# Rotary attention: the two value products of a key tile issued in one beat of every two instead of one in each

## The chip, the cores and the metric
The kernel runs on one core of a Trainium2 chip. The metric is the device time of one execution in microseconds (us); lower is better. Before the change three runs gave 2062.24, 2063.32 and 2064.73 us, median 2063.32 us.

## What is computed
The input x has 16 batches of 512 tokens with 128 features. Four blocks follow one another, each added to x: a causal attention, a feed-forward block, an attention with rotary positions ("rotary attention", the one that changes), and the same feed-forward block again. Each starts from a layer norm. The rotary attention is, cut to what matters:

```
q, k, v = (x @ Wq.T + bq), (x @ Wk.T + bk), (x @ Wv.T + bv)   # 16 heads of 8
q, k = rope(q, k)
scores = einsum('bhnd,bhmd->bhnm', q, k) / sqrt(8)
attn = softmax(scores)                        # no mask: all 512 x 512 of a head
out = einsum('bhnm,bhmd->bhnd', attn, v) @ Wo.T + bo
```

## The kernel before, in words
The whole of x stays on the chip. Each attention is a software pipeline over the batches: step n works on several batches at once, each in another stage. A step has 32 **beats** (`BEATS`, 4 groups of 4 heads times 8 beats). In every beat TensorE (PE) executes in the order given by `"order": "SMWX"`:

- S, `scores` (line 1007): the scores of batch n-2 for one pair of heads and one tile of 128 keys, two matmuls of 50 rows by 512 queries, side by side in the upper and the lower half of the array. Here they are called S(i,0) and S(i,1) for beat i. Each writes a PSUM bank of its own.
- M, `maxes` (line 1025): the same products the other way round for batch n-1, two matmuls, from which VectorE (DVE) takes the maxima over the keys (`max_of`, line 882).
- W, `weigh` (line 1065): a **value block**. Four matmuls, one for each head of the group, in four column strips of 32; each multiplies 128 keys of the probabilities (256 of the 512 queries) with the values and a column of ones (9 columns, float32), and adds to `ps_out`. Float32 matmuls stand as two records each in the trace, so a block is "x8".
- X, `misc_work`: at a few beats of a step, projections of q, k, v (lines 1106, 1109), the output product (line 1135), transposes of the normed x (line 1092) and of the maxima (line 1076).

ScalarE (ACT) takes the exponential of each score bank in order (line 993: two per beat, `prob`), and copies `ps_out` to SBUF once a group of heads is complete (`group_out`, line 956, `o_raw`).

The banks set the waits. The scores have `SCORE_BANKS = 3` banks, taken in turn by S(i,0), S(i,1), S(i+1,0), S(i+1,1) and so on (`act_bank_free`): so S(i+1,1) takes the bank of S(i,0) and waits for its exponential. Transposes at beats 3, 19 and 23 take turns too. The maxima have two pairs of banks: M of beat i waits for DVE's reduction of beat i-2. `ps_out` is one bank: the first value block of a group waits for the copy of the group before (`s["o_raw"]` in `weigh`). PE, ACT and DVE each execute their instructions in program order.

`ROTARY_AT` is the table that puts the parts at their beats. `"weigh"` gives, for the eight value blocks of a group G, the beat counted from 8G. Block 2j and block 2j+1 are the two halves of the queries (0 to 255, 256 to 511) of key tile j, and both read the probabilities of beats 2j and 2j+1; beats past 31 fall in the next step. There are 8 probability buffers (`PROBS`): the exponential of beat i waits for the last block that reads beat i-8.

Of the kernel before, what the change touches and what calls it, by code (L numbers as in the profile page):

```python
# [328 lines left out]
def norm_apply(dve, m, s, b):  # L329
# [3 lines left out]
    for t in range(T):  # L333
# [7 lines left out]
             "P_nm0": 10, "P_o": 1, "D_stats": 6, "D_clear": 9, "D_q": 14, "D_k": 4, "A_v": 6, "D_bias": 6, "D_inv": 12,  # L341
             "D_proj": 9, "A_nm1": 2, "A_nm0": 14, "A_xT": 10, "order": "MSWX"}
ROTARY_AT = {"k": 3, "nm1": 3, "v": 15, "proj": 14, "xT": 19, "nm0": 23, "q": 23,
             "weigh": (4, 5, 6, 7, 8, 9, 10, 11), "out": 12, "P_nm1": 8, "P_norm": 15, "P_v": 13, "P_bias": 15,
             "P_q1": 27, "P_q2": 31, "P_k1": 9, "P_k2": 13, "P_nm0": 19, "P_o": 0, "D_stats": 16, "D_clear": 18,
             "D_q": 24, "D_k": 4, "A_v": 16, "D_bias": 2, "D_inv": 15, "D_proj": 15, "A_nm1": 4,
             "A_nm0": 24, "A_xT": 20, "order": "SMWX"}
# [1291 lines left out]
```

## Time and profile before
| | |
|---|---|
| median of three runs | 2063.32 us |
| the profiled execution, its time | 2065.22 us |
| its span on the chip | 2063.5 us |
| granted TensorE clock, mean over the span | 0.962 |
| rotary attention in the main loop | about 995 to 1697 us |
| one step of it (one batch) | 43.4 us |
| busy over the span | PE 92%, DVE 83%, ACT 72%, POOL (GpSimd) 57% |

An engine's busy time is the union of its instructions. Matmuls are pipelined, and the end of each is modelled, so the distance between the starts of two instructions says more than the length of one. Idle time in brackets stands before an instruction, with what released it. Step n of the rotary loop does the scores for batch n-2: steps 2 to 16 have S, M and W, step 17 has S and W alone, and the next feed-forward block begins beside it.

### The profile page before, as it was taken

The page shows a single profiled execution, that of the slowest core. Times are in us where ns is not written, and L with a number is a line of the kernel's source. Part 1 is how long each engine was busy: PE and PEld are TensorE (multiplying, and loading weights), DVE is VectorE, ACT ScalarE, POOL GpSimd, SP SyncE. Part 2 cuts the span into 40 slices and gives each one's busy share as a digit, 9 for nine tenths or more (in the row PEclk, how much of TensorE's full clock was granted, in tenths as well). Part 3 has the DMA queues.
Part 4 walks back from the last instruction along what each step waited for, and adds up shares of the span by engine and source line. Part 5 has one row for each costly group of instructions (what it writes and reads, how often), then busy time and mean ns, then how long its engine had stood idle before and what let it go on. Part 6 is the DMA issues. An engine that isn't in the chain of part 4 may idle for free.

```text
span 2063.5 us, 42740 instructions
## 1 busy us (share of the span) xinstructions
PE 1888.6 (92%) x16132; PEld 966.2 (47%) x16132; DVE 1702.8 (83%) x2312; ACT 1478.0 (72%) x2641; POOL 1175.8 (57%) x1615
## 2 busy tenths in 40 slices
PE   3899999999889999986899999999999989999998
PEld 1333444444357777764222222222222227777776
DVE  4889898898658888876899999999999918888883
ACT  1478788788756666652698888888888876666665
POOL 6777788877446555677444454454553015555654
PEclk6799999999989999998799999999999989999999
DMA  7455656655110000014334444444444010000000
GB/s 180 99 120 134 131 125 140 126 121 119 25 40 1 0 1 1 1 27 101 88 90 101 99 105 107 95 100 95 101 111 95 14 19 12 11 16 11 11 16 16
DMA packets 107892, 144.81 MB, mean 70 GB/s; under 512 B 19105, under 2 KB 87458, under 8 KB 101538
## 3 DMA queue, kind: packets, MB, share of 16 engines
q1 hardware_dynamic: 107682, 142.01, 30.3%
q8 instruction: 132, 2.16, 0.5%
q14 instruction: 78, 0.64, 0.1%
HBM read 67.52 MB, written 55.58 MB: 60 GB/s over the span
## 4 chain that ended last, share of the span: by engine, by line
PE 59%; POOL 15%; issue 8%; ACT 8%; DVE 6%; DMA 2%; SPq 1%; POOLq 0%; another core or an unknown queue 0%; ACTq 0%; DVEq 0%
PE ps_score L1446 21%; PE ps_out L1065 12%; PE ps_score L1007 7%; ACT prob L993 6%; PE ps_max L1446 5%; PE ps_max L1025 5%; DVE negmax L882 3%; POOL xhat L324 3%; POOL prob L728 3%; PE ps_out L1446 3%; PE ps_max L1106 2%; POOL rstd L318 2%; POOL rest L693 1%; ACT o_raw L956 1%; POOL parts L700 1%
## 5 line engine op out<-in xcount | busy, mean ns | idle before, releaser
L993 ACT ACTIVATE prob<-ps_score 128x512 f32<-128x512 f32 x1664 | 900.4, 598 | 171.8 <-PE ps_score L1007 151.4
L882 DVE TENSOR_REDUCE negmax<-ps_max 128x2 f32<-128x1024 f32 (+1 forms) x896 | 905.6, 1066 | 90.7 <-PE ps_max L1042 47.9
L1065 PE MATMUL ps_out<-prob,v_aug 128*9 128x256 f32 (+2 forms) x6656 | 508.9, 386 | 30.9 <-ACT o_raw L956 20.4
L1446 PE MATMUL ps_score<-h,w_hi 128*128 128x512 f32 x2048 | 502.8, 399 | 9.4 <-POOL h L1224 8.2
L1446 PEld LDWEIGHTS ps_score<-h,w_hi 128*128 128x128 f32 x2048 | 383.3, 189 | 104.3 <-POOL h L1224 10.8
L1025 PE MATMUL ps_max<-stack_k,stack_q 48*128 48x512 bf16 (+3 forms) x2048 | 342.6, 353 | 46.6 <-DVE negmax L882 29.3
L1007 PE MATMUL ps_score<-stack_q,stack_k 50*128 50x512 bf16 (+3 forms) x2048 | 351.6, 347 | 31.0 <-ACT prob L993 23.1
L1212 POOL TENSOR_TENSOR h<-h3f,h 128x512 fp32r<-128x512 f32 x128 | 192.5, 1514 | 127.9 <-ACT h L1358 127.8
L728 POOL TENSOR_SCALAR_AFFINE_SELECT prob<-prob 128x256 f32<-128x256 f32 (+1 forms) x448 | 187.8, 440 | 117.7 <-ACT prob L993 117.3
L1065 PEld LDWEIGHTS ps_out<-prob,v_aug 128*9 128x9 f32 x6656 | 105.8, 89 | 306.0 <-ACT prob L993 153.9
L1007 PEld LDWEIGHTS ps_score<-stack_q,stack_k 50*128 50x128 bf16 x2048 | 103.7, 93 | 273.1 <-ACT prob L993 201.6
L1212 POOL TENSOR_TENSOR h<-h2f,h 128x512 fp32r<-128x512 f32 x128 | 172.7, 1351 | 68.3 <-ACT h L1358 68.3
L680 POOL TENSOR_TENSOR turned<-turned,rope 128x512 f32<-128x512 f32 x31 | 39.5, 1275 | 283.2 <-DMA turned<-qf 283.2
L1025 PEld LDWEIGHTS ps_max<-stack_k,stack_q 48*128 48x128 bf16 x2048 | 87.7, 95 | 200.8 <-DVE negmax L882 97.3
L1352 ACT ACTIVATE h3f<-ps_score,s_col 128x512 f32<-128x512 f32 x128 | 87.7, 685 | 110.8 <-PE ps_score L1446 104.2
L1352 ACT ACTIVATE h2f<-ps_score,s_col 128x512 f32<-128x512 f32 x128 | 88.2, 689 | 96.2 <-PE ps_score L1446 89.6
L1266 DVE CAST h<-h1f 128x512 fp32r<-128x512 f32 x120 | 124.9, 1041 | 37.5 <-PE ps_score L1446 36.4
L1446 PE MATMUL ps_max<-ffn_xT,w_hi 128*128 128x512 f32 x512 | 144.9, 415 | 3.4 <-DVE ffn_xT L1273 2.5
L334 DVE TENSOR_SCALAR xhat<-x,mv,rstd 128x128 f32<-128x128 f32 x128 | 95.5, 806 | 44.1 <-POOL rstd L306 44.1
L1253 DVE SCALAR_TENSOR_TENSOR ut<-tanh,ps_max 128x512 f32<-128x512 f32 x128 | 87.0, 680 | 53.1 <-ACT tanh L1369 50.6
L1268 DVE TENSOR_TENSOR h<-h1f,h 128x512 fp32r<-128x512 f32 x120 | 114.8, 957 | 4.1
L1446 PEld LDWEIGHTS ps_max<-ffn_xT,w_hi 128*128 128x128 f32 x512 | 93.4, 193 | 36.4 <-DVE ffn_xT L1273 15.5
(116 smaller groups left out, 2129.5 us busy)
## 6 DMA issues: line engine op xcount, KB each, us to landing
d_stack<-parts SPq DMA_DIRECT2D x64, 384.0 KB, 2.6
stack_q<-d_stack SPq DMA_DIRECT2D x64, 384.0 KB, 5.7
stack_k<-d_stack SPq DMA_DIRECT2D x64, 384.0 KB, 6.0
d_stack<-parts SPq DMA_DIRECT2D x64, 256.0 KB, 2.9
d_stack<-parts SPq DMA_DIRECT2D x64, 128.0 KB, 2.7
o_num<-o_raw SPq DMA_DIRECT2D x128, 64.0 KB
o_rden<-d_rden SPq DMA_DIRECT2D x128, 64.0 KB
turned<-qf SPq DMA_DIRECT2D x64, 128.0 KB, 2.4
```

The source lines that it names most:

```text
L334: last = dve.tensor_scalar(m["xhat"][:, t, :], m["x"][:, b % B, t, :], m["mv"][:, t, 0:1], m["rstd"][:, t:t + 1], ALU.subtract, ALU.mult)
L728: last = pool.affine_select(out=tri, in_=tri, compare_op=ALU.is_ge, fill=0.0, base=0, pattern=[[0, tri.shape[1]], [1, P]], channel_multipl ...
L882: last = dve.tensor_reduce(m["negmax"][:, t, :, p], banks[:, :, at:at + w], AX.X, ALU.max, negate=True)
L993: act.activation(prob(b, i)[:, o], act_bank("score", 2 * i + o), ACT.Exp).then_inc(s["prob"], 1)
L1007: mm = pe.matmul(act_bank("score", 2 * i + o)[:, at:at + w], m["stack_k"][c][rows, p, P * j:P * (j + 1)], m["stack_q"][c][rows, p, S - w:S ...
L1025: last = pe.matmul(to[:, o, at:at + w], m["stack_q"][c][rows, p, P * t:P * (t + 1)], m["stack_k"][c][rows, p, 0:w], start=(piece == 0), st ...
L1065: last = pe.matmul(m["ps_out"][32 * g:32 * g + HD + 1, out:out + w], m["v_aug"][b % VALUES][:, j, 4 * G + g, :], prob(b, beat)[:, g % 2, l ...
L1212: pool.tensor_tensor(h[k][:, 1, f], hf[k][:, f % 2], h[k][:, 0, f], ALU.subtract).then_inc(s[f"h{k}"], 1)
L1266: dve.tensor_copy(h[1][:, 0, f], h1f[:, f % 2]).then_inc(s["h1_hi"], 1)
L1268: dve.tensor_tensor(h[1][:, 1, f], h1f[:, f % 2], h[1][:, 0, f], ALU.subtract).then_inc(s["h1"], 1)
L1352: act.activation(hf[k][:, f % 2], m["ps_hid"][:, f % 2], ACT.Gelu, scale=m["s_col"][:, k, f:f + 1]).then_inc(s[f"h{k}f"], 1)
L1446: mm = pe.matmul(to, w[:, cols], moving(part), start=begin and i == 0, stop=last and i == len(pairs) - 1)
```

## The change
One row of the table:

```diff
 ROTARY_AT = {"k": 3, "nm1": 3, "v": 15, "proj": 14, "xT": 19, "nm0": 23, "q": 23,
-             "weigh": (4, 5, 6, 7, 8, 9, 10, 11), "out": 12, "P_nm1": 8, "P_norm": 15, "P_v": 13, "P_bias": 15,
+             "weigh": (5, 5, 7, 7, 9, 9, 11, 11), "out": 12, "P_nm1": 8, "P_norm": 15, "P_v": 13, "P_bias": 15,
              "P_q1": 27, "P_q2": 31, "P_k1": 9, "P_k2": 13, "P_nm0": 19, "P_o": 0, "D_stats": 16, "D_clear": 18,
```

The even blocks (0, 2, 4, 6) of each group go one beat later, behind S and M of the odd beat, directly in front of the odd block, which stays. Even beats have S and M (and X) alone; odd beats have S, M and two value blocks. The number of instructions of each kind stays. A group's first block goes from beat 8G+4 to beat 8G+5; the last one stays at 8G+11, and the copy of a group's output stays at ACT's beat 8G+12.

## Rows read from the trace of the kernel before
**Rows 1.** The page's first part: busy us (share of the span) xinstructions.
```profile
PE 1888.6 (92%) x16132; PEld 966.2 (47%) x16132; DVE 1702.8 (83%) x2312; ACT 1478.0 (72%) x2641; POOL 1175.8 (57%) x1615
```
**Rows 2.** Busy time by stretch, one step: PE, PEld, DVE, ACT, POOL, clock, DMA share, GB/s.
```profile
1306.82:1350.27 43.45, 41.14 (x418) 11.71 (x416) 40.41 (x45) 38.25 (x73) 21.34 (x28) 1.00 0.46 101
```
**Rows 3.** Who waited for whom, 1306.33 to 1349.79: us in total, times, longest.
```profile
ACT prob L993 <- PE ps_score L1007: 3.1, 5, 1.1
...
PE ps_out L1065 <- ACT o_raw L956: 1.4, 3, 0.6
...
PE ps_score L1007 <- ACT prob L993: 0.6, 1, 0.6
...
PE ps_score L1092 <- POOL xhat L324: 0.4, 1, 0.4
```
**Rows 4.** Order of time, PE, beats 4 and 5: start, length, instruction.
```profile
1306.33 0.39 PE L1007 MATMUL ps_score<-stack_q,stack_k 50*128 50x512 bf16 x2
1306.56 0.38 PE L1025 MATMUL ps_max<-stack_k,stack_q 48*128 48x512 bf16 x2
1306.87 0.62 PE L1065 MATMUL ps_out<-prob,v_aug 128*9 128x256 f32 x8
1307.42 0.43 PE L1007 MATMUL ps_score<-stack_q,stack_k 50*128 50x512 bf16 x2
...
1308.00 0.62 PE L1065 MATMUL ps_out<-prob,v_aug 128*9 128x256 f32 x8
1308.55 0.39 PE L1007 MATMUL ps_score<-stack_q,stack_k 50*128 50x512 bf16 x2
```
**Rows 5.** Order of time, ACT, beats 4 to 11.
```profile
1306.82 8.84 ACT L993 ACTIVATE prob<-ps_score 128x512 f32<-128x512 f32 x16 [0.36 <-PE ps_score L1007]
```
**Rows 6.** Order of time, beats 16 and 17, after the v projection.
```profile
1322.23 0.39 PE L1007 MATMUL ps_score<-stack_q,stack_k 50*128 50x512 bf16 x2
...
1322.83 2.06 ACT L993 ACTIVATE prob<-ps_score 128x512 f32<-128x512 f32 x4
...
1323.32 0.54 PE L1007 MATMUL ps_score<-stack_q,stack_k 50*128 50x512 bf16 x2
...
1324.01 0.62 PE L1065 MATMUL ps_out<-prob,v_aug 128*9 128x256 f32 x8
```
**Rows 7.** Order of time, PE after the loop: four value blocks with nothing between.
```profile
1693.73 1.91 PE L1065 MATMUL ps_out<-prob,v_aug 128*9 128x256 f32 x32
...
1695.57 1.20 PE L1446 MATMUL ps_max<-ffn_xT,w_hi 128*128 128x512 f32 x4
```
**Rows 8.** Order of time, beats 11 to 14, around a group's copy.
```profile
1314.67 0.62 PE L1065 MATMUL ps_out<-prob,v_aug 128*9 128x256 f32 x8
...
1315.54 0.60 ACT L956 ACTIVATE o_raw<-ps_out 128x512 f32<-128x512 f32 x1
...
1316.20 0.62 PE L1065 MATMUL ps_out<-prob,v_aug 128*9 128x256 f32 x8 [0.37 <-ACT o_raw L956]
...
1317.84 0.43 PE L1007 MATMUL ps_score<-stack_q,stack_k 50*128 50x512 bf16 x2
```
**Rows 9.** Order of time, PE, output product of beat 14, scores of 15.
```profile
1318.97 1.16 PE L1135 MATMUL ps_max<-weights,oT 128*128 128x128 f32 x8
...
1320.06 0.39 PE L1007 MATMUL ps_score<-stack_q,stack_k 50*128 50x512 bf16 x2
```
**Rows 10.** Order of time, PE, the first scores of the next step.
```profile
1344.10 0.39 PE L1007 MATMUL ps_score<-stack_q,stack_k 50*128 50x512 bf16 x2 [0.56 <-ACT prob L993]
```
**Rows 11.** Order of time, DVE, ten reductions on end.
```profile
1350.56 11.52 DVE L882 TENSOR_REDUCE negmax<-ps_max 128x2 f32<-128x1024 f32 x10
```
**Rows 12.** Order of time, PE, a beat of step 17 (no M).
```profile
1645.44 0.63 PE L1007 MATMUL ps_score<-stack_q,stack_k 50*128 50x512 bf16 x2
```
**Rows 13.** Order of time, PE at the lower clock, S of two successive beats.
```profile
1001.76 0.61 PE L1007 MATMUL ps_score<-stack_q,stack_k 50*128 50x512 bf16 x2
...
1003.70 0.61 PE L1007 MATMUL ps_score<-stack_q,stack_k 50*128 50x512 bf16 x2
```

## The prediction
> **What bounds the kernel now.** I read the page's busy shares first: PE leads with 92% of the span [rows 1]. The diff touches only the rotary attention, so next I read one step of it in the view by stretches: of 43.45 us PE is busy 41.14, DVE 40.41, ACT 38.25, at a granted clock of 1.00, the level of 2.4 GHz [rows 2]. Three engines are within 3 us of each other, so a share says little about which sets the pace; the order of time has to. The waits of one step are small: ACT waits 3.1 us for scores, PE 1.4 us for group copies, 0.6 us for an exponential at the step's start, 0.4 us for the normed x [rows 3].
>
> In the order of time a plain beat on PE is S to M 0.23, M to W 0.31, W to the next S 0.55; two beats take 1308.55 - 1306.33 = 2.22 us [rows 4]. A second loop is as long, and the view of waits hardly shows it. S(4,0) starts at 1306.33, its exponential at 1306.82, 0.49 later [rows 4, 5]. An exponential lasts 0.60. S(5,1) takes the bank of S(4,0): its exponential ends at 1306.82 + 0.60 = 1307.42, and S of beat 5, started at 1307.42, is 0.43 long where its neighbours are 0.39: its second matmul came 0.04 later [rows 4]. So the loop "S(i,0), its exponential, S(i+1,1)" takes 0.49 + 0.60 + 0.04, about 1.12 us, whatever PE does in between. Beats 16 and 17 prove it: the exponential of S(16,0) is held back by the v copy to 1322.83 and ends at 1323.43; S(17,0) starts at 1323.32, S ends 0.15 later than usual (0.54 against 0.39), so S(17,1) started about 1323.47, 0.04 after that end, and W of the beat went with it, to 1324.01, 0.54 after S(17,1) [rows 6]. A beat that lacks M shows the same: S is 0.63 long, 0.24 of it waiting [rows 12].
>
> **The change part by part.** No instruction is added or removed.
>
> *The even beat loses its value block (0.55 us).* S(e,0) at 0, M at 0.23, S(o,0) at about 0.45. S(o,1) then waits for the exponential of S(e,0): it cannot start before 1.12. M of the odd beat and both value blocks stand behind it on PE. So of the 0.55 us taken out here nothing is gained; the even beat's distance to S(o,1) stays 1.12 to 1.13 (today 1307.46 - 1306.33).
>
> *The odd beat has two value blocks.* From S(o,1) to the first W 0.54 [rows 4, 6]. Two blocks on end are not in a rotary beat of the trace. The nearest row: four on end take 1695.57 - 1693.73 = 1.84, that is 0.43 each and 0.12 once for the way out of them [rows 7]; two are 0.98. From below I take 0.86 (the way out hidden), from above two single ones, 2 x 0.55 = 1.10. I take 0.98, the same operation in the same shapes.
>
> *A plain pair of beats* is then 1.12 + 0.54 + 0.98 = 2.64 us (2.52 to 2.76) against 2.22: **+0.41**. The 0.12 that adjacency saves goes under the wait. At the pair's end: the four exponentials follow one another 0.49 apart (four in 2.06, [rows 6]) from 0.48, and end at 2.55, before the next S at 2.64, whose first exponential starts at 3.12. DVE needs 1.15 a beat (ten in 11.52, [rows 11]), 2.30 a pair, and is not late. 16 pairs a step: +6.6 us.
>
> *What goes back.* (a) The group copies. The first block of a group now comes a beat after the copy's place, so PE's wait at it goes: 1.4 us in three, at beats 12, 20 and 28 [rows 3]. But the copy sits in front of the exponential of the even beat, and begins 0.25 us after W has ended (1314.67 + 0.62 to 1315.54, [rows 8]): from the next S that is 0.32, plus 0.48 for the copy, so the exponential starts at 0.80 and not 0.48, and the loop carries these 0.32. Today the pair of beats 12 and 13 is 1317.84 - 1315.22 = 2.62 (1315.22 is W at 1314.67 and 0.55); it becomes 2.96. That is +0.34 and not +0.41, for three pairs -0.2. (b) The output product in beat 14, 1.09 us from 1318.97 to 1320.06 [rows 9], falls in an even beat, where PE is waiting: S(15,0) at 0.23 + 0.31 + 1.09 = 1.63 instead of 1.12, so it costs 0.51 of its 1.09: -0.58. (c) At the step's start S(0,0) waits for the last exponential of beat 31, 0.56 on PE [rows 10]. The pair of beats 30 and 31 is now longer than its exponentials (2.55, and 0.15 from the end to S), so 0.5 of that wait is swallowed: -0.5. (d) The wait for the normed x, 0.4 [rows 3], ends by POOL's own work, which the change does not lengthen; PE arrives later: -0.4. All other X work stands behind odd beats and is added to a pair as before. What is late next after (a) and (c) is the same exponential of the even beat. SP, the DMAs and POOL keep their order; no instruction passes another there, and with POOL at 21.34 of 43.45 [rows 2] a longer step gives them room.
>
> A step: 6.6 - 0.2 - 0.6 - 0.5 - 0.4 = **+4.9**, nearer to +4.8 with unrounded terms; 43.4 becomes 48.2.
>
> *All steps.* Steps 3 to 14: 12 x 4.8 = 57.6. Step 2 has 14 such pairs: +4.0. Steps 15 and 16 have no transpose of x, so (d) is missing: 2 x 5.2. Step 17 has no M: a pair becomes 2.64 - 0.22 = 2.42 against at most 2.24 (two turns of the loop) and about 2.0 where the beats run by PE; over 14 pairs +2.5 to +5.9, part of it under waits there: I take +4. The sum is +76 us. The profiled execution took 2065.22 us (span 2063.5); it becomes 2141. Against the median of 2063.32 that is 2139 us.
>
> *The clock.* Today PE has 2.3 us idle in a step at a granted 1.00 [rows 2]; it will have some 0.3 us idle in each pair, 4 to 5 us more in a step. At the lower level a rotary beat takes 1003.70 - 1001.76 = 1.94 us [rows 13], so a pair would be about 4.0 against 2.64. No stretch of the rotary loop shows the clock falling at such gaps, and gaps below 1 us stand in it at 1.00; I cost it at nothing in the forecast and keep it as a rival.
>
> **The rivals.**
>
> *The clock falls (slower still).* If PE, with a gap in each pair, spends a tenth to a quarter of the loop at 1.2 GHz, then each low pair costs 1.36 us more: 250 pairs x 1.36 x 0.1 to 0.25 = +34 to +85, so 2173 to 2224 us. For it: the gaps come regularly. Against: each is short, and PE is still busy about 89%. The Trainium skill, page "TensorE: Matmul & The Clock Gate", section "A second HAM failure mode: psum-queue depth-cycling", describes just this pattern, 512-column bf16 matmuls that cycle through PSUM banks with small idle times between groups, and says that the clock then swings between its two levels. The present loop cycles three banks at 1.00 [rows 2], so the trace does not bear the rule out at today's gaps; at the new ones no row shows it.
>
> *Adjacency saves nothing:* two blocks take 1.10, a pair 2.76, and +0.12 x 250 = +30: 2169 us. Against it stand rows 7.
>
> *PE alone sets the pace (faster).* If S(o,1) did not have to wait, a pair on PE would be 0.22 + 0.22 + 0.22 + 0.31 + 0.98 = 1.95, and DVE would bound it with 2.30. The waits for group copies and the step's start go too; a step is then DVE's 40.41 busy and about 1 us that it still waits for q, 41.4 instead of 43.4: -2.0 in 15.5 steps, -31 us, 2032 us. It decides from the point where the exponential of S(e,0) is over when S(o,0) is issued, at 0.45. For it: PE leads the busy shares, and 0.12 us goes at each way out of the value blocks. Against: that exponential ends at 1.08, by rows 4 to 6.
>
> *The value blocks' place does not matter* (the wait for the bank is in fact shorter, and a pair stays about 2.22 to 2.30): -0.1 to +0.5% of the time, near 2063. Against it the same rows.
>
> **How the numbers follow.** Forecast 0.78; clock 0.08; no saving 0.05; PE sets the pace 0.06; no matter 0.03. The forecast's own range: the value blocks 0.86 to 1.10, so ±0.12 x 250 = ±30, and step 17 ±2; the upper side meets the rival with 1.10. I take 2112 to 2170, which leaves out the faster cases and the worse half of the clock's. A change of 0.2% (4 us) is about what can be told from none. Faster by more 0.07, within 0.02, slower 0.91.
>
> **What would show it.** Right: rotary steps of 48.2 us (47 to 50); on ACT, groups of four exponentials, 2.07 long, with about 0.57 idle before each for scores; on PE, S of odd beats held by ACT's exponential for some 0.3 us, fifteen times a step, and x16 value groups 0.98 from start to next S; no wait of a value block for the group copy; DVE idle about 7 us in a step; clock 1.00. Wrong: exponentials without a gap, or a step under 43.4 (the bank wait does not bind), a granted clock under 0.98 in the loop (the clock rival), x16 groups of 1.10.

## The result and the profile after
The changed kernel takes 2144.61 us (median of four runs, 2144.46 to 2144.65) against 2064.03 us for the kernel before beside it: the ratio is 1.0391, 95% interval 1.0377 to 1.0405. It is 80.6 us slower; 2139 us were forecast, in a range of 2112 to 2170. The span of the profiled execution went from 2063.5 to 2142.7 us.

First the page's busy shares, which answer to [rows 1], and the view by stretches for one step, from one v copy to the next, which answers to [rows 2].

```profile
PE 1914.8 (89%) x16132; PEld 1004.8 (47%) x16132; DVE 1716.2 (80%) x2312; ACT 1462.5 (68%) x2641; POOL 1178.0 (55%) x1615
...
1067.77:1116.01 48.24, 42.73 (x418) 14.20 (x417) 41.12 (x43) 37.24 (x73) 21.37 (x28) 1.00 0.39 89
```

A step has the same 418 matmul records and takes 48.24 us instead of 43.45. The busy times move by 1.6 us at most; what grew is the idle time of each engine: PE from 2.3 to 5.5 us, DVE from 3.0 to 7.1, ACT from 5.2 to 11.0. They do not stand together: PE is busy while ACT waits for it, and ACT while PE waits. The waits of the same step, to be read beside [rows 3]:

```profile
ACT prob L993 <- PE ps_score L1007: 7.7, 13, 0.8
PE ps_score L1007 <- ACT prob L993: 5.4, 15, 0.6
DVE negmax L882 <- PE ps_max L1025: 5.0, 15, 0.9
```

PE and ACT wait for each other: PE 15 times a step for an exponential (5.4 us; it was 0.6), ACT 7.7 us for scores (it was 3.1). DVE waits 5.0 us for the products M. The wait of a value block for a group copy, 1.4 us in [rows 3], is gone. The order of time shows one pair of beats; it answers to [rows 4].

```profile
1392.95 0.39 PE L1007 MATMUL ps_score<-stack_q,stack_k 50*128 50x512 bf16 x2
1393.17 0.38 PE L1025 MATMUL ps_max<-stack_k,stack_q 48*128 48x512 bf16 x2
1393.39 0.38 PE L1007 MATMUL ps_score<-stack_q,stack_k 50*128 50x512 bf16 x1
1393.43 2.06 ACT L993 ACTIVATE prob<-ps_score 128x512 f32<-128x512 f32 x4 [0.59 <-PE ps_score L1007]
1393.60 2.36 DVE L882 TENSOR_REDUCE negmax<-ps_max 128x2 f32<-128x1024 f32 x2 [0.30 <-PE ps_max L1025]
1394.08 0.39 PE L1007 MATMUL ps_score<-stack_q,stack_k 50*128 50x512 bf16 x1 [0.31 <-ACT prob L993]
1394.09 0.60 PE L1025 MATMUL ps_max<-stack_k,stack_q 48*128 48x512 bf16 x2
1394.62 1.05 PE L1065 MATMUL ps_out<-prob,v_aug 128*9 128x256 f32 x16
1395.60 0.39 PE L1007 MATMUL ps_score<-stack_q,stack_k 50*128 50x512 bf16 x2
```

Read it down. S of the even beat at 1392.95, S(o,0) at 1393.39, and S(o,1), a group of its own now, at 1394.08: the view puts 0.31 idle before it and names the exponential. The first exponential began at 1393.43 and ended 0.60 later, at 1394.03. From S(e,0) to S(o,1) it is 1.13. Two value blocks follow at +0.54, and the next S 0.98 after them, so adjacency does save its 0.12. The pair is 1395.60 - 1392.95 = 2.65. ACT has groups of four exponentials with 0.59 idle before each, where [rows 5] has sixteen on end.

### The profile page after: what moved, and what is told of

Its sections match the earlier page's. It is cut to its first block, busy times and chain, and to the rows that moved or that the text cites. A ratio compares the mean times of both kernels' runs of the same rounds, so it can differ in the third digit from the quotient of the medians.

```text
span 2142.7 us, 42740 instructions
## 1 busy us (share of the span) xinstructions
PE 1914.8 (89%) x16132; PEld 1004.8 (47%) x16132; DVE 1716.2 (80%) x2312; ACT 1462.5 (68%) x2641; POOL 1178.0 (55%) x1615
## 4 chain that ended last, share of the span: by engine, by line
PE 66%; POOL 11%; ACT 10%; issue 7%; DVE 4%; DMA 1%; SPq 0%; POOLq 0%; ACTq 0%; DVEq 0%
PE ps_score L1446 20%; PE ps_out L1065 16%; PE ps_score L1007 10%; ACT prob L993 8%; PE ps_max L1446 5%; PE ps_max L1025 5%; POOL prob L728 3%; PE ps_max L1106 2%; PE ps_out L1446 2%; DVE negmax L882 2%; POOL xhat L324 1%; ACT o_raw L956 1%; POOL rest L693 1%; POOL parts L700 1%; POOL rstd L318 1%
## 5 line engine op out<-in xcount | busy, mean ns | idle before, releaser
L993 ACT ACTIVATE prob<-ps_score 128x512 f32<-128x512 f32 x1664 | 877.2, 603 | 234.3 <-PE ps_score L1007 224.2
L882 DVE TENSOR_REDUCE negmax<-ps_max 128x2 f32<-128x1024 f32 (+1 forms) x896 | 921.0, 1067 | 133.1 <-PE ps_max L1025 83.1
L1007 PE MATMUL ps_score<-stack_q,stack_k 50*128 50x512 bf16 (+3 forms) x2048 | 426.0, 347 | 109.4 <-ACT prob L993 100.2
L1065 PE MATMUL ps_out<-prob,v_aug 128*9 128x256 f32 (+2 forms) x6656 | 465.0, 387 | 9.6 <-POOL prob L728 9.6
L1025 PE MATMUL ps_max<-stack_k,stack_q 48*128 48x512 bf16 (+3 forms) x2048 | 379.8, 352 | 46.8 <-DVE negmax L882 30.2
L1007 PEld LDWEIGHTS ps_score<-stack_q,stack_k 50*128 50x128 bf16 x2048 | 114.5, 94 | 391.0 <-ACT prob L993 302.0
L1065 PEld LDWEIGHTS ps_out<-prob,v_aug 128*9 128x9 f32 x6656 | 132.3, 90 | 232.2 <-issue 81.3
```

The source lines that it names most:

```text
L882: last = dve.tensor_reduce(m["negmax"][:, t, :, p], banks[:, :, at:at + w], AX.X, ALU.max, negate=True)
L993: act.activation(prob(b, i)[:, o], act_bank("score", 2 * i + o), ACT.Exp).then_inc(s["prob"], 1)
L1007: mm = pe.matmul(act_bank("score", 2 * i + o)[:, at:at + w], m["stack_k"][c][rows, p, P * j:P * (j + 1)], m["stack_q"][c][rows, p, S - w:S ...
L1025: last = pe.matmul(to[:, o, at:at + w], m["stack_q"][c][rows, p, P * t:P * (t + 1)], m["stack_k"][c][rows, p, 0:w], start=(piece == 0), st ...
L1065: last = pe.matmul(m["ps_out"][32 * g:32 * g + HD + 1, out:out + w], m["v_aug"][b % VALUES][:, j, 4 * G + g, :], prob(b, beat)[:, g % 2, l ...
```

## The experiments
Each was timed beside the kernel before on its own chip; the medians of before were 2061.3 and 2061.4 us there. Ratios are to these. "Step" is the mean of 13 steps, from one v copy to the next.

| kernel | us | ratio, 95% interval | step, us |
|---|---|---|---|
| before | 2064.03 | | 43.46 |
| changed | 2144.61 | 1.0391 (1.0377 to 1.0405) | 48.24 |
| e1, changed, S(o,1) behind M | 2100.02 | 1.0193 (1.0176 to 1.0210) | 45.42 |
| e2, before, S(i,1) behind M | 2060.30 | 0.9992 (0.9982 to 1.0001) | 43.25 |
| e3, pairs in the even beat | 2154.31 | 1.0454 (1.0433 to 1.0476) | 48.66 |
| e4, one pair in four | 2086.30 | 1.0122 (1.0105 to 1.0139) | 45.16 |
| e5, before, short exponentials | 2043.63 | 0.9914 (0.9898 to 0.9931) | 42.54 |
| e6, changed, short exponentials | 2071.81 | 1.0049 (1.0032 to 1.0065) | 43.62 |
| e7, changed, last batch as before | 2132.30 | 1.0352 (1.0335 to 1.0369) | |
| e8, before, last batch in pairs | 2071.81 | 1.0050 (1.0033 to 1.0066) | |

**e1: what stands behind the wait.** The theory: the loop from S(e,0) over its exponential to S(o,1) holds its length, and everything PE has behind S(o,1) is added. The rival: two value blocks on end are the cost. The order in which the four matmuls of S and M are issued tells them apart. The edit in words:

```diff
-    S(i,0), S(i,1), M(upper half), M(lower half)      # scores(), then maxes()
+    S(i,0), M(lower half), M(upper half), S(i,1)      # one function, steps 2 to 16
```

> The changed kernel, with the four matmuls of S and M of a beat in another order: S(i,0), M for the lower half, M for the upper half, S(i,1). Same work, same banks. Theory (the loop S(e,0), its exponential, S(o,1) holds 1.12 us of the pair, and what stands behind S(o,1) on PE is added to it): M of the odd beat no longer stands behind the wait, so from S(o,1) to the first value block it is 0.22 + 0.10 = 0.32 instead of 0.53, a pair is 1.12 + 0.32 + 0.98 = 2.42 instead of 2.65, a step 48.2 - 16 x 0.22 = 44.7, and the kernel 2145 - 54 = about 2090 us (2080 to 2105). Rival (two value blocks on end are themselves what costs, or the waits come from ACT's own throughput): the order of S and M does nothing, 2140 to 2148.

2100.02 us: 2% of the time came back by an order alone. In the order of time of e1 (line 1057 is S, 1068 M, 1092 the value blocks):

```profile
1211.65 0.39 PE L1057 MATMUL ps_score<-stack_q,stack_k 50*128 50x512 bf16 x1
...
1212.79 0.39 PE L1057 MATMUL ps_score<-stack_q,stack_k 50*128 50x512 bf16 x1
1213.10 1.05 PE L1092 MATMUL ps_out<-prob,v_aug 128*9 128x256 f32 x16
1214.09 0.39 PE L1057 MATMUL ps_score<-stack_q,stack_k 50*128 50x512 bf16 x1
```

S(e,0) to S(o,1) is 1.14, nearly the 1.13 of the changed kernel, then 0.31 to the value blocks instead of 0.54, 0.99 to the next S: a pair of 2.44 (2.42 expected). The total is 10 us above the expected 2090. One pair of a step accounts for some 4 of them: where the next step begins and waits for the last exponential, S stands at 1216.66 and 1219.36, 2.70 apart. Another 6 stand in the pair of beats 14 and 15 (S at 1192.38 and 1196.91, 4.53 apart), which was to become 0.22 shorter than the 4.32 of the changed kernel and became 0.21 longer; why was not taken apart.

**e2: the same order without the change.**

> The kernel before, with the same order S(i,0), M lower, M upper, S(i,1) in a beat. Theory: S(i,1) comes 0.22 later without holding anything, so the bank wait (0.04 every second beat, 0.15 after the v copy) goes, and a plain beat is 1.09 on PE; DVE needs 1.15 a beat and then sets the pace in parts: a step of 42.5 to 43.2 instead of 43.4, 2050 to 2062 us, most likely 2055. Rival (PE alone sets the pace today): no change, 2064.

2060.30 us lies in the expected range and is also not told from no change, so the time decides nothing. The order of time does: the bank wait did go. S stands every 1.09 us (1306.08, 1307.17, 1308.26) where [rows 4] alternates between 1.09 and 1.13. After five such intervals M comes 0.04 behind S and the beats are 1.12 again, DVE's pace, and the group copy stops PE as before:

```profile
1305.77 11.41 DVE L882 TENSOR_REDUCE negmax<-ps_max 128x2 f32<-128x1024 f32 x10
...
1314.76 0.62 PE L1092 MATMUL ps_out<-prob,v_aug 128*9 128x256 f32 x8 [0.33 <-ACT o_raw L956]
```

DVE's ten reductions take 11.41 us, PE's ten beats would take 10.9. What the bank loop gave up, DVE took over. So the loop and DVE were nearly level before the change: shortening the loop brings nothing to be seen in the time, lengthening it does.

**e3: the pairs in the even beat.** `weigh` at (4, 4, 6, 6, 8, 8, 10, 10).

> Both value blocks of a key tile in the even beat instead of the odd one: weigh at (4, 4, 6, 6, 8, 8, 10, 10). Theory: a pair keeps its 2.64, with the waiting now in the odd beat, where the X work of beats 3, 15, 19 and 23 falls into it: some 0.55 to 0.69 us hidden in each of four, 2.3 us a step; back come the output product of beat 14 (0.58), the wait for the group copy (0.35 net in a step) and the wait at the step's start (0.55). A step of about 47.4 instead of 48.2, 2145 - 12 = about 2132 us (2120 to 2142). Rival (adjacent blocks cost wherever they stand, nothing is hidden in the gap): 2145 or, with the copy's wait back, above.

A miss: 2154.31 us, and a step of 48.66 instead of 47.4. By the time alone the rival, in which nothing is hidden and the copy's wait comes back, would be right; the rows show that work is hidden, but too little of it. A plain pair is again 2.65, so the place of the doubled beat does not matter, as the theory has it. But the gap hid less X work than I had put down, and the waits that come back are longer. Rows of e3 for the step's start, a group's first blocks and the v projection:

```profile
1237.03 0.39 PE L1007 MATMUL ps_score<-stack_q,stack_k 50*128 50x512 bf16 x2
...
1239.02 0.39 PE L1007 MATMUL ps_score<-stack_q,stack_k 50*128 50x512 bf16 x2 [1.38 <-ACT prob L993]
...
1256.85 1.05 PE L1065 MATMUL ps_out<-prob,v_aug 128*9 128x256 f32 x16 [0.37 <-ACT o_raw L956]
...
1261.57 0.39 PE L1007 MATMUL ps_score<-stack_q,stack_k 50*128 50x512 bf16 x2
...
1262.42 1.16 PE L1109 MATMUL ps_max<-weights,xT 128*128 128x128 f32 x8 [0.24 <-DVE x L896]
1263.51 0.39 PE L1007 MATMUL ps_score<-stack_q,stack_k 50*128 50x512 bf16 x2
```

From the S of beat 31 to that of beat 0 it is 1.99 us where the loop alone would need 1.13: 0.86 and not 0.55 for the step's start. The wait for a group copy, 0.37, makes the pair of beats 12 and 13 3.10 long instead of 2.79, 0.3 for one copy where 0.35 was put down for a whole step. Around the v projection S to S is 1.94: 0.81 of its 1.09 stays on the path and 0.28 is hidden, not the 0.6 expected. The missing 0.3 is a wait inside the gap: from M to the projection it is 0.62, with 0.24 named as DVE's residual, where the changed kernel has 0.32 from M to the output product. The gap itself holds more: of the work at beat 3 (S at 1243.19 and 1245.11, 1.92 apart) 0.79 stays on the path, where it adds 1.26 to a pair of the changed kernel, so 0.47 is hidden, and the same at beat 23. With 0.18 at beat 19 that makes 1.4 us a step, not 2.3.

**e4: a dose.** `weigh` at (5, 5, 6, 7, 8, 9, 10, 11): four pairs a step instead of sixteen.

> Only the first two blocks of a group are put together: weigh at (5, 5, 6, 7, 8, 9, 10, 11). Theory: four pairs of a step instead of sixteen lengthen, three of them those behind a group's copy: 3 x 0.34 + 0.41 = 1.43 us a step, 15.4 steps, +22: about 2086 us (2080 to 2092). Rival (the wait for the group copy, 1.4 us a step in the kernel before, is real loss and goes with the first block's move, and one late block of four is absorbed by the others): 2045 to 2064.

2086.30 us, with 2086 expected; to the kernel before on its chip it is +25, with +22 expected. The group copies' wait of the kernel before is therefore no free gain for a late first block. Part of the +25 is not the loop's. Ten of the 13 steps take 44.3 to 45.1 us, mostly 44.80, but three take 46.3, and each of these holds a stretch at the lower clock. The view by stretches around the first (the clock is the third number from the end):

```profile
1109.00:1112.40 3.40, 2.39 (x20) 0.85 (x20) 2.22 (x3) 2.81 (x7) 2.02 (x4) 1.00 1.02 207
1112.40:1115.80 3.40, 3.40 (x28) 0.62 (x20) 1.86 (x2) 1.78 (x4) 0.00 (x0) 0.50 0.14 22
```

In the 3.4 us before it fell PE had waited for the normed x and then up to 0.59 us for an exponential. The three together are 4.5 us, so in the profiled execution the pairs account for some 21 of the 25 us.

**e5 and e6: a shorter loop.** In both the exponential of the rotary attention takes 128 of its 512 columns and the value products read those 128 twice, so the rotary attention's output is another; all banks and waits stay.

The edit, without the one in the value products:

```diff
-                act.activation(prob(b, i)[:, o], act_bank("score", 2 * i + o), ACT.Exp)
+                w = S if causal else S // 4
+                act.activation(prob(b, i)[:, o, 0:w], act_bank("score", 2 * i + o)[:, 0:w], ACT.Exp)
```

> The kernel before, but in the rotary attention an exponential takes only the first 128 of its 512 columns, and the value products read these 128 twice over: the output of the rotary attention is not the reference's, all instructions, banks and waits stay. An exponential falls from 0.60 to some 0.25 us (not under 0.60 - 0.75 x 0.49 = 0.23). Theory: the bank loop falls from 1.12 to about 0.78; a beat is then bound by PE (1.09) and DVE (1.15); the wait at the step's start (0.56) goes too. A step of about 42.3 instead of 43.4, 2064 - 16 = about 2048 us (2035 to 2060).

> The changed kernel with the same short exponentials (128 of 512 columns, read twice; the rotary attention's output is not the reference's). Theory (bank wait): S(o,1) can start 0.78 after S(e,0) at the latest, a pair is 1.95 on PE or 2.30 on DVE, and the grouping costs nothing more or brings a little: a step of 41.5 to 43, about 2038 us (2025 to 2060), so within 20 us of the kernel before with the same short exponentials instead of 80 above it. Rival (two value blocks side by side cost on PE by themselves, or the idle gaps do): it stays 60 to 80 us above that kernel.

2043.63 us is within its range. 2071.81 us is a miss: 2025 to 2060 was expected, at most 20 us above e5, and it is 28.2. Still, with the exponential shortened the same change costs 28.2 us instead of 80.6, and the rival's 60 to 80 is refuted. An exponential of e5, and a pair of e6 (lines 1009, 1067 and 994 are S, value blocks and the exponential):

```profile
1227.86 0.27 ACT L994 ACTIVATE prob<-ps_score 128x128 f32<-128x128 f32 x1
```

```profile
1208.39 0.39 PE L1009 MATMUL ps_score<-stack_q,stack_k 50*128 50x512 bf16 x2
...
1208.84 0.76 PE L1009 MATMUL ps_score<-stack_q,stack_k 50*128 50x512 bf16 x2
1208.88 1.03 ACT L994 ACTIVATE prob<-ps_score 128x128 f32<-128x128 f32 x4 [1.30 <-PE ps_score L1009]
...
1209.74 1.05 PE L1067 MATMUL ps_out<-prob,v_aug 128*9 128x256 f32 x16
1210.73 0.39 PE L1009 MATMUL ps_score<-stack_q,stack_k 50*128 50x512 bf16 x2
```

The loop becomes 0.49 + 0.27 + 0.04 = 0.80, and 0.80 + 0.54 + 0.98 = 2.32; the pair is 2.34. S(o,1) still comes 0.37 after S(o,0) (0.76 against 0.39), so the bank still binds a little. The exponential is 0.33 shorter, and the pair 0.31. The expectation took 1.95 on PE or 2.30 on DVE for a pair and held that the grouping would then cost nothing. The loop's own sum with its 0.78 is 2.30 too, and a pair of e5 is 2.18 (S every 1.09: 1228.30, 1229.38), so the grouping still costs 0.15 a pair; and the last step was not counted. Of the 28.2 us, the steps make 15 x (43.62 - 42.54) = 16; most of the rest stands at the end, where e6 takes 115.2 us and e5 105.1 from the last v copy to the first tanh (see e8).

**e7 and e8: the last step.** Step 17 (S and value blocks alone) took 9 us more, the forecast had 4. The view by stretches, step 17 of the changed kernel, then of the kernel before (from the first exponential of the step to the first tanh of the feed-forward block):

```profile
1715.98:1773.30 57.32, 43.96 (x317) 13.23 (x317) 6.17 (x19) 34.12 (x66) 4.26 (x7) 0.70 0.07 12
```

```profile
1645.04:1693.37 48.33, 38.68 (x337) 10.71 (x330) 7.07 (x26) 36.16 (x70) 5.49 (x8) 0.86 0.07 14
```

The granted clock is 0.70 instead of 0.86 over it. Both kernels wait there for POOL's parts of the maxima, first the changed kernel, then the one before:

```profile
1721.45 0.39 PE L1076 MATMUL ps_score<-ident_b,nm_parts 128*16 128x128 bf16 x4 [3.45 <-POOL nm_parts L667]
```

```profile
1652.84 0.59 PE L1076 MATMUL ps_score<-ident_b,nm_parts 128*16 128x128 bf16 x4 [4.21 <-POOL nm_parts L667]
```

PE falls to 1.2 GHz in both: for 23.9 us from 1722.2 in the changed kernel, for 10.2 us from 1650.5 in the one before (the expectation of e7 has 7). e7 is the changed kernel with the value blocks of the last batch one in each beat; e8 is the kernel before with those alone in pairs (the function they are in, cut):

```diff
+        last = [self.group * G + at for G in range(GROUPS) for at in (4, 5, 6, 7, 8, 9, 10, 11)]   # e8: (5, 5, 7, 7, 9, 9, 11, 11)
         return [(lag, k) for lag in (2, 3)
-                for k, at in enumerate(self.weigh_at)
+                for k, at in enumerate(last if self.rotary and n - lag == B - 1 else self.weigh_at)
                 if at == i + self.beats * (lag - 2)]
```

> The changed kernel, but the value blocks of the last batch (step 17, where M is missing, and the four behind it) stand one in each beat as before. In the changed kernel step 17 takes 57.3 us against 48.3, with the granted clock at 0.50 from about 1724 to 1745; before it was 0.50 for some 7 us. Theory A (the pairs of step 17 keep TensorE at its lower clock longer, and that is most of the 9 us): 0.50 for some 7 us again, 2145 - 8 = about 2137 us. Theory B (the long low clock comes from how step 16 ends and the wait after it): it stays, 2141 to 2145.

> The kernel before, with the value blocks of the last batch alone in pairs. Theory A: about 2064 + 8 = 2072 us, with the granted clock at 0.50 for some 20 us in step 17. Theory B: 2064 to 2068.

e8 is +10.4 us, ratio 1.0050 (1.0033 to 1.0066); its profiled execution, at 2075.69 the longest of the four, holds besides a step of 45.4 instead of 43.4 us with 3.4 us at 0.50 in it (from 1458.9), in a loop that e8 shares with the kernel before. e7's ratio is 0.0039 below that of the changed kernel, 8 us; from the last v copy to the first tanh it takes 115.7 us where the changed kernel takes 126.6. The clock stood at 0.50 for 6.8 us in e7 and, in two parts, for 20.5 in e8. This is theory A. Eight microseconds from 16 us after the step's start, PE, PEld, DVE, ACT, POOL and clock: changed, before, e8.

```profile
1731.98:1739.98 8.00, 7.36 (x48) 1.84 (x40) 0.00 (x0) 4.71 (x10) 0.00 (x0) 0.50 0.11 34
```

```profile
1661.04:1669.04 8.00, 6.92 (x72) 2.06 (x64) 0.00 (x0) 7.37 (x16) 0.00 (x0) 1.00 0.12 36
```

```profile
1661.00:1669.00 8.00, 7.23 (x52) 1.94 (x44) 0.00 (x0) 3.85 (x8) 0.00 (x0) 0.61 0.19 46
```

With single blocks PE has its 1.00 back by 16 us after the step's start; with pairs it has 1.00 for good only 30 (changed) and 32 us (e8) after it. At 1.2 GHz a pair there takes 3.71 us (exponentials of the changed kernel at 1726.53 and 1730.24). That the pairs hold the clock down is shown; what about them does it is not.

## Why the prediction was right
*The reading that decided it.* PE led with 95% busy in a step, and the change takes one of two ways in and out of the value blocks off PE in every pair. By the busy shares it should have been faster. The 0.04 by which every second S was late [rows 4], and beat 17 behind the v copy [rows 6], showed a loop over ACT and a bank that was as long as a beat. The even beat's block was work inside that loop, at no cost; moved behind it, it cost 0.43.

*The plain pair*, 2.64 forecast: measured 2.65, part by part (1.13, 0.54, 0.98). e1 changed the second part alone (2.44), e6 the first (2.34); both follow the sum within 0.02.

*The step*, 48.2 forecast: 48.24, but terms were off and cancelled; that it fits to 0.1 is luck. (a) The group copy: I put 0.32 on the loop for it, from the 0.25 between the end of W and the copy [rows 8]. The changed kernel has

```profile
1397.27 1.05 PE L1065 MATMUL ps_out<-prob,v_aug 128*9 128x256 f32 x16
1398.26 0.39 PE L1007 MATMUL ps_score<-stack_q,stack_k 50*128 50x512 bf16 x2
1398.39 0.60 ACT L956 ACTIVATE o_raw<-ps_out 128x512 f32<-128x512 f32 x1 [0.24 <-PE ps_out L1065]
...
1398.88 2.06 ACT L993 ACTIVATE prob<-ps_score 128x512 f32<-128x512 f32 x4
...
1401.05 0.39 PE L1007 MATMUL ps_score<-stack_q,stack_k 50*128 50x512 bf16 x2
```

the copy starts 0.07 after the blocks end, and the exponential 0.62, not 0.80, after S. The 0.25 of before was ACT's own queue: the sixteen exponentials of [rows 5] end at 1315.66, and the copy at 1315.54 was behind them. The pair is 2.79, not 2.96, at beats 12 and 28; at beat 20, where ACT copies the transposed x as well, it went from 2.88 to 3.26 (S at 1411.37 and 1414.63), about the +0.34 forecast. That is -0.3 in a step. Against it stand 0.01 to 0.02 on each plain pair, 0.2 in a step, and 0.1 on the pair of beats 14 and 15 (1401.05 to 1405.37, 4.32 where the forecast's terms give 2.64 + 0.51 + 1.09 = 4.24), where the output product cost 0.5 of its 1.09 as forecast:

```profile
1401.59 1.16 PE L1135 MATMUL ps_max<-weights,oT 128*128 128x128 f32 x8
...
1402.68 0.39 PE L1007 MATMUL ps_score<-stack_q,stack_k 50*128 50x512 bf16 x2
```

*The sum.* To the start of step 17 the kernel lost 1715.98 - 1645.04 = 70.9 us, with 72 forecast. Step 17 was mis-sized: +4 forecast, +9.0 measured; that is 5.0 of the 5.6 us between 2139 and the result. The step of the argument that failed is "the clock, I cost it at nothing": true of the loop of this kernel (1.00 from 1002 us, early in step 2, to 1722, with a gap of 0.31 in a plain pair), untrue in step 17, where a wait of 3.45 us came before the pairs. The rule that I had weighed, in the Trainium skill, page "TensorE: Matmul & The Clock Gate", section "A second HAM failure mode: psum-queue depth-cycling", that small gaps between bank-cycling groups make the clock swing, is not borne out by the loop's 1.00; of the last step, where a longer wait has first brought PE down, it tells nothing. But the loop is not out of the clock's reach: e4 and e8 show stretches of 3.4 us at 0.50 in it, 1.5 to 2 us each. The forecast kernel had none in its profiled execution, and no run shows what decides it.

*The rivals.* That PE alone sets the pace is refuted by the 0.31 wait in each pair and by e1 and e6, where the pair follows the loop. Whether the grouping would gain with no bank wait at all stays open: in e6 the bank still binds, and its pair is 2.34 where e5 has 2.18. No version with more score banks was run. That adjacency saves nothing is refuted by 0.98. That the place does not matter is refuted by the 80 us.

## What to carry to other kernels
Before moving work on the busiest engine, follow one buffer round: from its writer over its reader to the writer's next turn. If that loop is as long as the engine's own beat, the work inside the loop is free and the same work behind its wait is not, and the busy shares will not tell. In an in-order queue put the instruction that waits for such a buffer last in its group. The last was worth 2% in the changed kernel (e1) and nothing to be told from none in the kernel before (e2). No version here that computes the same beats the kernel before by more than its measurement can tell.

## What was not expected of the hardware
In step 17 PE waited 3.4 to 5.4 us for POOL, and TensorE fell to its lower clock, in all ten kernels. With one value block in each beat it was at 1.00 again by 16 us after the step's start (before, e7); with two in every second beat only after 30 and 32 us (changed, e8). By the first stretch at 0.50 the kernels part in the same way: 6.8 to 10.2 us in before, e2, e4, e5 and e7; 23.9 in the changed kernel, e1 and e6; 13.7 in e3 and in e8, which had 6.8 more after 3.4 us at 1.00. Pairs that lose nothing by the clock at its upper level can cost 8 to 10 us in such a place.
